# Product of probabilities and V over 64 rows at once, with V's second arrangement laid out by DMA

## The chip, the cores and the metric

One Trainium2 (trn2) chip, one of its cores. The metric is device time in microseconds (us) from the start to the end of one execution of the whole kernel.

## What is computed

The program is a chain of layers over `x` of 16 sequences x 256 tokens x 128 channels: an opening stage (a scan with an orthogonal product), a transformer of six layers, a multi-query attention, a state-space stage and a mixture of experts. Only the transformer is touched. The part of it around the change, cut to what matters:

```python
WINDOW, HEADS, DIM_HEAD, DEPTH = 32, 16, 64, 6
def local_attention(q, k, v):          # b, h, n, d ; n = 256 tokens
    bq, bk, bv = (t.reshape(b, h, n // 32, 32, d) for t in (q, k, v))
    look = lambda t: concat([block before (zeros ahead of the first), the block itself], axis=3)
    sim = einsum('bhwie,bhwje->bhwij', bq, look(bk)) * 8.0
    sim = where(it < jb or it > jb + 32 or no such block, -big, sim)
    return einsum('bhwij,bhwje->bhwie', softmax(sim), look(bv))
def attn_layer(x):                     # q, k: l2norm, rotary; v plain
    return local_attention(q, k, v) @ Wo
# each layer: x + attn_layer(shift_tokens(x)), then x + a gated feed-forward of 341 hidden columns
```

So each block of 32 queries looks at 64 keys: its own block of 32 and the one before it.

## The kernel before, in words

The transformer stage (`transformer_stage`, lines 780 to 1485) works on tiles of 128 tokens: 6 layers x 16 sequences x 2 tiles = 192 tiles. Sequence number and layer make a unit `U` (96 of them), `t` is the tile of a unit (0 is the even tile, 1 the odd one). The work is a software pipeline of steps, written out by hand in one `body` for each engine, in the same order of steps on all (`all_steps`, line 770). In step k tile k is projected to q and k, tile k-1 is turned, tile k-2 has its scores and V, tile k-3 its product with V, tile k-4 its output projection. Every fourth step ends a pair of units, and the feed-forward of an earlier pair is spread over the four steps (`ff`, 0 to 3). Everything is f32; a matmul in f32 is two instructions in the trace, each with a weight load of its own.

TensorE's order in a step (line 1207): `project(step, 0)` (L1071), with ff = 1 `turn_xn`, `scores` (L1102, L1112), with ff = 3 `widen(step, 2)`, `turn_probs` (L1053), `output` (L1167), `project(step, 1)`, `turn_part(step, 0)` (L1053, eight transposes of q), `attend(step, 0)`, `turn_part(step, 1)` (eight transposes of k), `attend(step, 1)`, `project_v` (L1087), in odd steps `turn_input`, and last `widen(step, 0)` with ff = 1, `widen(step, 1)` with ff = 2 (both L1189) or `narrow` with ff = 3 (L1203).

`attend` (line 1123) is what the change is about. V of a tile lies with its blocks of 32 keys in four places: block 2m + parity of the odd or even heads in partitions 64 odd + 32 parity, slot m. `V` has four such slots of tiles in a ring (`v_slot`, line 700), filled by ScalarE from PSUM (`keep_v`, L1275). The matmuls take 32 rows (the keys of one block), 64 weight columns (V's channels of one head) and 64 or 32 moving columns (the queries that look at this block), and add in the two PSUM banks `mixed`, which two bf16 matmuls with zero weights (L1131) clear first. `attend(step, 0)` does the blocks of parity 0, `attend(step, 1)`, after a wait for the first to be done, those of parity 1 and, in odd tiles, the last block of the tile before:

```python
windows = [(0, 0), (2, 0)]                                    # parity 0: 64 columns each
windows = [(1, 0), (3, 0)] + ([(3, 1)] if t else [])          # parity 1: 64, 32 (and 32) columns
r = slice(64 * odd + 32 * parity, 64 * odd + 32 * parity + 32)
```

ScalarE's order in a step (line 1319) ends with: `copy_part(step, 0)` (L1283), `square(step, 1)` (L1264), `copy_part(step, 1)` (L1283), `keep_out` (L1298: the result of `attend`, after both parities), `inverse_norm` (L1269, L1271), `keep_v` (L1275), in odd steps `copy_input` (L1259), then a gelu. `widen` with j < 2 and `narrow` write to the same banks `mixed` and so wait for `keep_out` (lines 1184 and 1195); the next step's `scores` wait for `keep_v`.

SyncE issues all DMAs of the stage from one queue in program order (lines 859 to 988): for each unit `residual(U)` (a wait for tile 2U-3's sum, then three shifting copies in SBUF, L897 to L899, and a load, L891) and `unit(U)` (weights at layer ends, `load_input` L886 to L888, every second unit `save_pair` L904).

Of the kernel before, what the change touches and what calls it, by code (L numbers as in the profile page):

```python
# [11 lines left out]
ACT = mybir.ActivationFunctionType  # L12
AX = mybir.AxisListType
F32 = mybir.dt.float32
BF16 = mybir.dt.bfloat16

P = 128
B = 16
T = 256
TT = T // P  # L20
# [641 lines left out]
PAIRS = HEADS // 2  # L662
# [24 lines left out]
class Step:  # L687
# [11 lines left out]

    def v_slot(self, lag):  # L700

        return (self.k - lag) % 4

# [76 lines left out]
def transformer_stage(k, z):  # L780

    nc, d = k.nc, k.dram
    with ExitStack() as ctx:
# [13 lines left out]
        identb = sb("identb", [P, P], BF16)  # L797
        zerob = sb("zerob", [P, P], BF16)

# [10 lines left out]
        kT = sb("kT", [P, PAIRS, WIN + T])  # L810
        V = sb("V", [P, 4, WPT // 2, PAIRS, HD])
        prob = sb("prob", [P, TT, PAIRS, 2, HD])
# [36 lines left out]
        clamped, logged, rn_ready = (ev(n) for n in "clamped logged rn_ready".split())  # L849
        v_done, v_kept, pv_done = ev("v_done"), ev("v_kept"), ev("pv_done", 2)  # L850
        scored, maxed, centred, exped, den_sum, den_inv, prob_ready, o_copied, out_done, z_added = (
# [7 lines left out]
        def _(sp):  # L859
            for e in (zu_ready, zr_ready[0], zr_ready[1], zsh_ready, z_saved, q_ok, k_ok, v_ok, out_ok, ff_ok):  # L860
                e.start(sp)
# [28 lines left out]
            def load_residual(u, p):  # L890
                sp.dma_start(zr[:, p, :, :], z[:, bass.ds(u * TT, TT), :]).then_inc(zr_ready[p].sem, 16)  # L891

            def shift_output(U, unit):
# [36 lines left out]
            def unit(U):  # L930


                nonlocal loads
                l, i, J = U // B, U % B, U // 2 - 2
                if i == B - 1 and l + 1 < DEPTH:
                    sp.wait_ge(roped.sem, roped.at(U * 2 + 1, 1))
                    load_columns(l + 1, 0)
                    load_table(l + 1, 0)
                    loads += 2
                    sp.wait_ge(weights, 16 * loads)  # L940
                sp.sem_inc(q_ok.sem, 1)
                if i == B - 1 and l + 1 < DEPTH:
                    sp.wait_ge(roped.sem, roped.at(U * 2 + 1, 2))
                    load_columns(l + 1, 1)
                    load_table(l + 1, 1)
                    loads += 2
                    sp.wait_ge(weights, 16 * loads)
                sp.sem_inc(k_ok.sem, 1)
                if i == 0 and l:
                    sp.wait_ge(v_done.sem, v_done.at(U * 2 - 1, 1))  # L950
                    load_columns(l, 2)
                    loads += 1
                    sp.wait_ge(weights, 16 * loads)
                if U:
                    sp.sem_inc(v_ok.sem, 1)
                if U + 2 <= UNITS:
                    sp.wait_ge(filled, place(Step(U * 2 // LOOP, U * 2 % LOOP + 1), "input") + 1)
                    load_input((i + 2) % B)
                if i % 2 and J >= 0:
                    save_pair(J % (B // 2), J)  # L960
                    if i == 3 and l:
                        load_ff_weights(l)
                        loads += 4
                        sp.wait_ge(weights, 16 * loads)
                    sp.sem_inc(ff_ok.sem, 1)
# [11 lines left out]

            for U in range(UNITS):
                if U >= 2:
                    residual(U)  # L980
                unit(U)
            for i in range(2):
                shift_output(UNITS + i - 2, i + 2)
                sp.sem_inc(out_ok.sem, 1)
# [62 lines left out]
        def _(pe):  # L1047
# [74 lines left out]

            def attend(step, parity):

                tau, t = step.tile(3), step.t(3)
                if parity == 0:
                    pe.wait_ge(copied, place(step, "p") + 2)
                    pe.wait_ge(v_kept.sem, v_kept.at(tau, 1))
                    pe.wait_ge(z_added.sem, z_added.at(tau - 1, 1))
                    for odd in range(2):  # L1130
                        nc.tensor.matmul(mixed[:, odd, 0:1], zerob[:, :], identb[:, 0:1],  # L1131
                                         start=True, stop=False, skip_group_check=True)
                    windows = [(0, 0), (2, 0)]
                else:
                    pe.wait_ge(pv_done.sem, pv_done.at(tau, 1))
                    windows = [(1, 0), (3, 0)] + ([(3, 1)] if t else [])
                for j in range(PAIRS // 2):
                    for v, back in windows:
                        lo, hi = (0, WIN) if back else (v * WIN, min(v + 2, WPT) * WIN)
                        for half in range(2):  # L1140
                            for odd in range(2):
                                r = slice(64 * odd + 32 * parity, 64 * odd + 32 * parity + 32)
                                pair = j + 4 * half
                                last = nc.tensor.matmul(mixed[64 * half:64 * half + 64, odd, j * P + lo:j * P + hi],  # L1144
                                                        V[r, step.v_slot(3 + back), v // 2, pair, :],
                                                        probT[r, t, pair, lo:hi],
                                                        start=False, stop=True, skip_group_check=True)
                last.then_inc(pv_done.sem, 1)
# [58 lines left out]
            def body(step):  # L1207
# [19 lines left out]
                if step.has(3):  # L1227
                    attend(step, 0)
                if step.has(1):
                    turn_part(step, 1)  # L1230
                if step.has(3):
                    attend(step, 1)
                if step.has(2):
# [10 lines left out]
            pe.wait_ge(zeroed, 5)  # L1244
            pe.wait_ge(masks_ready, 5)
            turn_input(0, 0)
# [4 lines left out]
        def _(act):  # L1251
# [20 lines left out]

            def keep_v(step):
                act.wait_ge(v_done.sem, v_done.at(step.tile(2), 1))
                nc.scalar.activation(V[:, step.v_slot(2), :, :, :].rearrange("p m a e -> p (m a e)"), flat2(score), ACT.Copy)\  # L1275
                    .then_inc(v_kept.sem, 1)
# [19 lines left out]
            def keep_out(step):  # L1296
                act.wait_ge(pv_done.sem, pv_done.at(step.tile(3), 2))
                nc.scalar.activation(oT[:, step.t(3), :, :], flat2(mixed).rearrange("p (a c) -> p a c", a=PAIRS),  # L1298
                                     ACT.Copy).then_inc(o_copied.sem, 1)
# [60 lines left out]
        def _(dve):  # L1360
# [6 lines left out]
            nc.vector.memset(eps[:, :], LN_EPS).then_inc(masks_ready, 1)  # L1367
            nc.vector.memset(zerob[:, :], 0.0).then_inc(masks_ready, 1)
            nc.vector.memset(ss[:, :, :, 1:2], 1e-24).then_inc(masks_ready, 1)
# [1456 lines left out]
```

## Time and profile before

| | us |
|---|---|
| median of 3 runs (lowest, highest) | 4871.99 (4866.45, 4878.07) |
| the profiled execution, its own time | 4863.11 |
| its span, first to last instruction | 4861.4 |
| TensorE (PE) busy | 4421.3 (91%) |
| VectorE (DVE) busy | 3153.7 (65%) |
| ScalarE (ACT) busy | 2729.3 (56%) |
| GpSimd (POOL) busy | 2625.0 (54%) |

The profile is of one execution. "Busy" is the union of an engine's instructions; PE is its matmuls, PEld its weight loads, which overlap them. Ends of matmuls are modelled, so a distance between two bursts is read from start to start. The transformer takes about the stretch from 200 to 3600 us of the span.

### The profile page before, as it was taken

The page shows a single profiled execution, that of the slowest core. Times are in us where ns is not written, and L with a number is a line of the kernel's source. Part 1 is how long each engine was busy: PE and PEld are TensorE (multiplying, and loading weights), DVE is VectorE, ACT ScalarE, POOL GpSimd, SP SyncE. Part 2 cuts the span into 40 slices and gives each one's busy share as a digit, 9 for nine tenths or more (in the row PEclk, how much of TensorE's full clock was granted, in tenths as well). Part 3 has the DMA queues.
Part 4 walks back from the last instruction along what each step waited for, and adds up shares of the span by engine and source line. Part 5 has one row for each costly group of instructions (what it writes and reads, how often), then busy time and mean ns, then how long its engine had stood idle before and what let it go on. Part 6 is the DMA issues. An engine that isn't in the chain of part 4 may idle for free. (4 is left out here: it accounts for less than half of the span.)

```text
span 4861.4 us, 165534 instructions
## 1 busy us (share of the span) xinstructions
PE 4421.3 (91%) x72708; PEld 2877.1 (59%) x72708; DVE 3153.7 (65%) x4106; ACT 2729.3 (56%) x3932; POOL 2625.0 (54%) x1465
## 2 busy tenths in 40 slices
PE   7489999999999999999999999999957999788868
PEld 5256666666666666666666666666634554344435
DVE  3477776767667676677666666667633333699964
ACT  4256665666566666656656665656632343577733
POOL 0266666666566665666656665666622111577742
PEclk8699999999999999999999999999987898899989
DMA  2100001000100001100010001100010000211100
GB/s 54 51 11 18 17 20 37 25 15 20 28 26 22 20 17 32 27 20 18 22 33 23 19 17 33 28 18 16 19 38 12 5 4 1 93 79 77 70 16 16
DMA packets 186590, 136.07 MB, mean 28 GB/s; under 512 B 122410, under 2 KB 172595, under 8 KB 183795
## 3 DMA queue, kind: packets, MB, share of 16 engines
q1 hardware_dynamic: 185843, 125.10, 8.6%
q8 instruction: 592, 9.70, 0.8%
q14 instruction: 155, 1.27, 0.1%
HBM read 68.51 MB, written 4.03 MB: 15 GB/s over the span
## 5 line engine op out<-in xcount | busy, mean ns | idle before, releaser
L1005 POOL TENSOR_TENSOR tf_qk<-tf_qk,tf_rot 128x1024 f32<-128x1024 f32 x384 | 908.7, 2366 | 1214.4 <-DVE tf_rot L1388 1214.4
L1071 PE MATMUL tf_psum<-tf_Wqkv,tf_xsT 128*128 128x512 f32 x1536 | 747.7, 610 | 66.2 <-issue 44.6
L1012 POOL TENSOR_TENSOR tf_qk<-tf_qk,tf_rn 128x1024 f32<-128x1024 f32 x384 | 724.2, 1912 | 55.3 <-ACT tf_rn L1271 55.3
L1264 ACT ACTIVATE tf_sq<-tf_psum 128x1024 f32<-128x1024 f32 x384 | 393.4, 1024 | 530.7 <-DVE tf_rot L1388 530.7
L1384 DVE TENSOR_TENSOR tf_qk<-tf_psum,tf_table 128x1024 f32<-128x1024 f32 x384 | 467.4, 1217 | 263.2 <-PE tf_psum L1071 262.6
L1144 PE MATMUL tf_psum<-tf_probT,tf_V 32*64 32x64 f32 (+1 forms) x27648 | 493.5, 219 | 7.2 <-issue 6.6
L1071 PEld LDWEIGHTS tf_psum<-tf_Wqkv,tf_xsT 128*128 128x128 f32 x1536 | 274.0, 194 | 349.0 <-issue 338.6
L1394 DVE TENSOR_REDUCE tf_ss<-tf_sq 128x16 f32<-128x1024 f32 x384 | 457.5, 1191 | 21.8 <-ACT tf_sq L1264 21.8
L1144 PEld LDWEIGHTS tf_psum<-tf_probT,tf_V 32*64 32x64 f32 x27648 | 442.8, 133 | 45.8 <-issue 41.0
L1388 DVE TENSOR_TENSOR tf_rot<-tf_psum,tf_table 128x1024 f32<-128x1024 f32 x384 | 465.8, 1213 | 0.0
L1053 PE MATMUL tf_psum<-ident,tf_qk 128*128 128x128 f32 x3072 | 409.5, 276 | 3.4 <-ACT tf_qT L1283 2.4
L1053 PEld LDWEIGHTS tf_psum<-ident,tf_qk 128*128 128x128 f32 x3072 | 344.0, 142 | 102.9 <-issue 82.2
L1447 DVE SCALAR_TENSOR_TENSOR tf_hT<-tf_psum,tf_b,tf_gel 128x512 f32<-128x512 f32 x144 | 107.4, 746 | 436.5 <-ACT tf_gel L1316 436.5
L1167 PE MATMUL tf_psum<-tf_Wo,tf_oT 128*128 128x128 f32 x3072 | 376.4, 275 | 8.2 <-issue 5.2
L1167 PEld LDWEIGHTS tf_psum<-tf_Wo,tf_oT 128*128 128x128 f32 x3072 | 362.3, 192 | 33.4 <-issue 22.9
L1020 POOL TENSOR_TENSOR tf_prob<-tf_prob,tf_rden 128x1024 f32<-128x1024 f32 x192 | 367.0, 1911 | 13.0 <-DVE tf_rden L1418 13.0
L1087 PE MATMUL tf_psum<-tf_Wqkv,tf_xsT 128*32 128x512 f32 x3072 | 369.6, 598 | 0.0
L1283 ACT ACTIVATE tf_qT<-tf_psum 128x1024 f32<-128x1024 f32 x192 | 196.4, 1023 | 282.0 <-PE tf_psum L1053 282.0
L2024 POOL TENSOR_TENSOR mb_read<-mb_state,mb_Csb 128x1024 f32<-128x1024 f32 x128 | 300.2, 2356 | 76.5 <-DVE mb_state L2267 57.0
L1112 PEld LDWEIGHTS tf_psum<-tf_kT,tf_qT 64*32 64x32 f32 x24576 | 261.0, 105 | 108.3 <-issue 108.0
L1112 PE MATMUL tf_psum<-tf_kT,tf_qT 64*32 64x64 f32 x24576 | 296.8, 226 | 20.6 <-issue 20.4
L2107 PE MATMUL mb_psum<-mb_read,ident 128*128 128x512 f32 x512 | 251.8, 615 | 59.3 <-POOL mb_read L2024 48.4
(313 smaller groups left out, 7542.0 us busy)
## 6 DMA issues: line engine op xcount, KB each, us to landing
mb_Csb<-mb_kept SPq DMA_DIRECT2D x16, 2048.0 KB, 7.1
tf_zr<-z SPq DMA_DIRECT2D x96, 128.0 KB, 2.7
z<-tf_z SPq DMA_DIRECT2D x48, 256.0 KB, 2.5
tf_Wqkv<-in_Wqkv_split SPq DMA_DIRECT2D x18, 512.0 KB, 3.7
tf_zu<-z SPq DMA_DIRECT2D x97, 64.0 KB
tf_zu<-z SPq DMA_DIRECT2D x97, 63.5 KB
tf_zsh<-tf_z SPq DMA_DIRECT2D x96, 64.0 KB
tf_zsh<-tf_z SPq DMA_DIRECT2D x96, 63.5 KB
```

The source lines that it names most:

```text
L1005: nc.gpsimd.tensor_tensor(v, v, rot[:, kind, :], ALU.add).then_inc(added.sem, 1)
L1012: nc.gpsimd.tensor_tensor(v, v, rn[:, t, HEADS * kind:HEADS * (kind + 1)].unsqueeze(2) .to_broadcast([P, HEADS, HD]), ALU.mult).then_inc(n ...
L1053: last = nc.tensor.transpose(flat2(trans)[:, j * P:(j + 1) * P], source(j), k.ident[:, :])
L1071: last = nc.tensor.matmul(proj[:, half, :], xsT[:, step.unit(0), WIN + t * P:WIN + (t + 1) * P], Wqkv[:, c:c + 512], start=True, stop=True)
L1087: last = nc.tensor.matmul(score[r:r + 32, m, :], xsT[:, step.unit(2), x:x + WIN], Wqkv[:, c:c + 512], start=True, stop=True)
L1112: last = nc.tensor.matmul(score[w * WIN:(w + 1) * WIN, odd, pair * HD:(pair + 1) * HD], qT[r, t, pair, w * WIN:(w + 1) * WIN], keys, start ...
L1144: last = nc.tensor.matmul(mixed[64 * half:64 * half + 64, odd, j * P + lo:j * P + hi], V[r, step.v_slot(3 + back), v // 2, pair, :], probT ...
L1167: last = nc.tensor.matmul(mixed[:, 0, 0:P], oT[:, t, pair, :], Wo[:, pair, :], start=(pair == 0), stop=(pair == PAIRS - 1))
L1264: nc.scalar.activation(sq[:, kind, :], flat2(proj), ACT.Square).then_inc(squared.sem, 1)
L1384: nc.vector.tensor_tensor(qk[:, t, kind, :].rearrange("p (h e) -> p h e", e=HD), v, cos, ALU.mult)
L1388: nc.vector.tensor_tensor(rot[:, kind, :].rearrange("p (h a e) -> p h a e", a=2, e=HD // 2), swapped, sin, ALU.mult).then_inc(roped.sem, 1)
L1394: nc.vector.tensor_reduce(ss[:, t, HEADS * kind:HEADS * (kind + 1), 0], sq[:, kind, :].rearrange("p (h e) -> p h e", e=HD), AX.X, ALU.add)\
```

## The change

Each block of queries now gets one matmul over both of its blocks of keys, 64 rows with 32 moving columns, written to PSUM at once instead of added there. For odd blocks of queries the two blocks of keys already lie side by side in `V`. For even ones a second arrangement, `Vback`, is filled by DMA from `V`: SyncE copies the rows of the block itself and, shifted by one slot, those of the block before (four DMAs for an even tile, six for an odd one: two of 128 KB, two or four of 64 KB). The first block of a sequence (w = 0, t = 0) has no block before it and keeps a matmul of 32 rows. The order of the probabilities' halves is as it was (the mask rolls them for even blocks). `V` has two slots in place of four, `Vback` two. The two halves of `attend` become one, between the two `turn_part`s. One bf16 matmul with the identity as weights stands ahead of it in place of two with zeros.

```diff
-        V = sb("V", [P, 4, WPT // 2, PAIRS, HD])
+        V, Vback = (sb(n, [P, TT, WPT // 2, PAIRS, HD]) for n in ("V", "Vback"))
...
+            def lay_back(tau):
+                t = tau % 2
+                sp.wait_ge(v_kept.sem, v_kept.at(tau, 1))
+                sp.wait_ge(pv_done.sem, pv_done.at(tau - 2, 1))
+                for odd in range(2):
+                    even_rows, odd_rows = (slice(64 * odd + i, 64 * odd + i + WIN) for i in (0, WIN))
+                    sp.dma_start(Vback[even_rows, t, :, :, :], V[even_rows, t, :, :, :]).then_inc(laid[t].sem, 16)
+                    sp.dma_start(Vback[odd_rows, t, 1, :, :], V[odd_rows, t, 0, :, :]).then_inc(laid[t].sem, 16)
+                    if t:
+                        sp.dma_start(Vback[odd_rows, 1, 0, :, :], V[odd_rows, 0, 1, :, :]).then_inc(laid[1].sem, 16)
...
                 if U:
                     sp.sem_inc(v_ok.sem, 1)
+                if U:
+                    lay_back(U * 2 - 1)
                 if U + 2 <= UNITS:
...
             for U in range(UNITS):
+                if U:
+                    lay_back(U * 2 - 2)
                 if U >= 2:
                     residual(U)
                 unit(U)
+            lay_back(TILES - 2)
+            lay_back(TILES - 1)
...
-            def attend(step, parity):
+            def attend(step):
...
+                pe.wait_ge(copied, place(step, "p") + 2)
+                pe.wait_ge(laid[t].sem, laid[t].at(step.unit_of(3), 96 if t else 64))
+                pe.wait_ge(z_added.sem, z_added.at(tau - 1, 1))
+                nc.tensor.matmul(mixed[:, 0, 0:1], identb[:, :], identb[:, 0:1], start=True, stop=True)
                 for j in range(PAIRS // 2):
-                    for v, back in windows:
-                        lo, hi = (0, WIN) if back else (v * WIN, min(v + 2, WPT) * WIN)
+                    for w in range(WPT):
+                        alone = w == 0 and t == 0
+                        source = Vback if w % 2 == 0 and not alone else V
                         for half in range(2):
                             for odd in range(2):
-                                r = slice(64 * odd + 32 * parity, 64 * odd + 32 * parity + 32)
-                                pair = j + 4 * half
-                                last = nc.tensor.matmul(mixed[64 * half:64 * half + 64, odd, j * P + lo:j * P + hi],
-                                                        V[r, step.v_slot(3 + back), v // 2, pair, :],
-                                                        probT[r, t, pair, lo:hi],
-                                                        start=False, stop=True, skip_group_check=True)
+                                r = slice(64 * odd, 64 * odd + (WIN if alone else 2 * WIN))
+                                pair, at = j + 4 * half, w * WIN
+                                last = nc.tensor.matmul(mixed[64 * half:64 * half + 64, odd, j * P + at:j * P + at + WIN],
+                                                        source[r, t, w // 2, pair, :], probT[r, t, pair, at:at + WIN],
+                                                        start=True, stop=True)
                 last.then_inc(pv_done.sem, 1)
...
                 if step.has(3):
-                    attend(step, 0)
+                    attend(step)
                 if step.has(1):
                     turn_part(step, 1)
-                if step.has(3):
-                    attend(step, 1)
...
             def keep_v(step):
+                t = step.t(2)
                 act.wait_ge(v_done.sem, v_done.at(step.tile(2), 1))
+                act.wait_ge(laid[1 - t].sem, laid[1 - t].at(step.unit_of(3), 64 if t else 96))
+                act.wait_ge(pv_done.sem, pv_done.at(step.tile(4), 1))
```

## Rows read from the trace of the kernel before

**Rows 1.** The page: the span, then busy time of each engine.
```profile
span 4861.4 us, 165534 instructions
...
PE 4421.3 (91%) x72708; PEld 2877.1 (59%) x72708; DVE 3153.7 (65%) x4106; ACT 2729.3 (56%) x3932; POOL 2625.0 (54%) x1465
```

**Rows 2.** Busy time by stretch, four of 700 us from 600 to 3400: their sum.
```profile
sum 2800.00, PE 2720.90 PEld 1872.19 DVE 1944.13 ACT 1703.77 POOL 1738.87; mean PE 680.23 PEld 468.05 DVE 486.03 ACT 425.94 POOL 434.72
```

**Rows 3.** Waits, PE alone, 600 to 3400: who, for whom, us in total, times, longest.
```profile
PE tf_psum L1071 <- issue: 25.1, 10, 3.5
...
PE tf_psum L1131 <- DVE tf_z L1429: 15.2, 41, 0.4
```

**Rows 4.** Groups by form, whole span: rows*columns of weights, moving operand, count | busy, mean ns.
```profile
L1144 PE MATMUL tf_psum<-tf_probT,tf_V 32*64 32x64 f32 x18432 | 451.0, 224 | 3.5 <-issue 3.3
...
L1144 PE MATMUL tf_psum<-tf_probT,tf_V 32*64 32x32 f32 x9216 | 238.1, 209 | 3.7 <-issue 3.2
...
L1131 PE MATMUL tf_psum<-tf_identb,tf_zerob 128*128 128x1 bf16 x384 | 36.6, 165 | 18.0 <-DVE tf_z L1429 18.0
```

**Rows 5.** Timeline of PE, parts of three steps: start us, length us, what, count.
```profile
2026.08 1.09 PE L1053 MATMUL tf_psum<-ident,tf_qk 128*128 128x128 f32 x8
2027.10 1.60 PE L1144 MATMUL tf_psum<-tf_probT,tf_V 32*64 32x64 f32 x96
2028.63 1.92 PE L1087 MATMUL tf_psum<-tf_Wqkv,tf_xsT 128*32 128x512 f32 x16
...
2036.93 1.95 PE L1167 MATMUL tf_psum<-tf_Wo,tf_oT 128*128 128x128 f32 x16
2038.72 1.88 PE L1071 MATMUL tf_psum<-tf_Wqkv,tf_xsT 128*128 128x512 f32 x4
...
2041.43 1.16 PE L1144 MATMUL tf_psum<-tf_probT,tf_V 32*64 32x64 f32 x64
2042.59 1.09 PE L1053 MATMUL tf_psum<-ident,tf_qk 128*128 128x128 f32 x8
2043.61 1.13 PE L1144 MATMUL tf_psum<-tf_probT,tf_V 32*64 32x64 f32 x64
2044.67 1.92 PE L1087 MATMUL tf_psum<-tf_Wqkv,tf_xsT 128*32 128x512 f32 x16
2046.53 0.44 PE L1053 MATMUL tf_psum<-ident,tf_zu 128*128 128x128 f32 x2
...
2048.52 1.88 PE L1071 MATMUL tf_psum<-tf_Wqkv,tf_xsT 128*128 128x512 f32 x4
2050.24 0.59 PE L1102 MATMUL tf_psum<-tf_mask,tf_identb 128*128 128x512 bf16 x2
```

**Rows 6.** Timeline of PE in the later stage of multi-query attention.
```profile
4000.06 0.40 PE L1653 MATMUL mq_psum<-mq_bv,mq_ones 1*128 1x32 f32 x2
4000.40 0.41 PE L1652 MATMUL mq_psum<-mq_Wv,mq_hT 128*128 128x32 f32 x2
4000.74 0.40 PE L1653 MATMUL mq_psum<-mq_bv,mq_ones 1*128 1x32 f32 x2
```

**Rows 7.** Timeline of ACT in the step of rows 5, and PE's next product.
```profile
2044.03 1.02 ACT L1283 ACTIVATE tf_kT<-tf_psum 128x1024 f32<-128x1024 f32 x1
2044.94 1.03 ACT L1298 ACTIVATE tf_oT<-tf_psum 128x1024 f32<-128x1024 f32 x1
...
2046.66 1.02 ACT L1275 ACTIVATE tf_V<-tf_psum 128x1024 f32<-128x1024 f32 x1 [0.31 <-PE tf_psum L1087]
...
2057.71 1.16 PE L1144 MATMUL tf_psum<-tf_probT,tf_V 32*64 32x64 f32 x64
```

**Rows 8.** DMA: two issues on SyncE's queue, and the page's line on `zr` (KB, landing).
```profile
2007.61 0.65 SPq L897 DMA_DIRECT2D tf_zsh<-tf_z  x1
...
2009.05 2.92 SPq L899 DMA_DIRECT2D tf_zsh<-tf_z  x1
...
tf_zr<-z SPq DMA_DIRECT2D x96, 128.0 KB, 2.7
```

More of the change, by code:

```diff
@@ L698, in t, with unit_of @@
         return (self.k - lag) % TT
-    def v_slot(self, lag):
-        return (self.k - lag) % 4
+    def unit_of(self, lag):
+        return self.I * (LOOP // 2) + (self.k - lag) // 2
     def unit(self, lag):
@@ L797, in transformer_stage @@
         identb = sb("identb", [P, P], BF16)
-        zerob = sb("zerob", [P, P], BF16)
         zu = sb("zu", [P, TT, P])
@@ L849, in transformer_stage @@
         clamped, logged, rn_ready = (ev(n) for n in "clamped logged rn_ready".split())
-        v_done, v_kept, pv_done = ev("v_done"), ev("v_kept"), ev("pv_done", 2)
+        v_done, v_kept, pv_done, laid = ev("v_done"), ev("v_kept"), ev("pv_done"), [ev("laid0", 64), ev("laid1", 96)]
         scored, maxed, centred, exped, den_sum, den_inv, prob_ready, o_copied, out_done, z_added = (
@@ L859, in _ @@
         def _(sp):
-            for e in (zu_ready, zr_ready[0], zr_ready[1], zsh_ready, z_saved, q_ok, k_ok, v_ok, out_ok, ff_ok):
+            for e in (zu_ready, zr_ready[0], zr_ready[1], laid[0], laid[1], zsh_ready, z_saved, q_ok, k_ok, v_ok, out_ok, ff_ok):
                 e.start(sp)
@@ L1121, in turn_probs @@
                 turn(PAIRS, lambda j: prob[:, t, j, :, :].rearrange("p b e -> p (b e)")).then_inc(filled, 1)
-            def attend(step, parity):
+            def attend(step):
                 tau, t = step.tile(3), step.t(3)
[L1126 to L1136, printed above, removed]
+                pe.wait_ge(copied, place(step, "p") + 2)
+                pe.wait_ge(laid[t].sem, laid[t].at(step.unit_of(3), 96 if t else 64))
+                pe.wait_ge(z_added.sem, z_added.at(tau - 1, 1))
+                nc.tensor.matmul(mixed[:, 0, 0:1], identb[:, :], identb[:, 0:1], start=True, stop=True)
@@ L1244, in _ @@
             pe.wait_ge(zeroed, 5)
-            pe.wait_ge(masks_ready, 5)
+            pe.wait_ge(masks_ready, 4)
             turn_input(0, 0)
@@ L1273, in keep_v @@
             def keep_v(step):
+                t = step.t(2)
                 act.wait_ge(v_done.sem, v_done.at(step.tile(2), 1))
-                nc.scalar.activation(V[:, step.v_slot(2), :, :, :].rearrange("p m a e -> p (m a e)"), flat2(score), ACT.Copy)\
+                act.wait_ge(laid[1 - t].sem, laid[1 - t].at(step.unit_of(3), 64 if t else 96))
+                act.wait_ge(pv_done.sem, pv_done.at(step.tile(4), 1))
+                nc.scalar.activation(V[:, t, :, :, :].rearrange("p m a e -> p (m a e)"), flat2(score), ACT.Copy)\
                     .then_inc(v_kept.sem, 1)
@@ L1296, in keep_out @@
             def keep_out(step):
-                act.wait_ge(pv_done.sem, pv_done.at(step.tile(3), 2))
+                act.wait_ge(pv_done.sem, pv_done.at(step.tile(3), 1))
                 nc.scalar.activation(oT[:, step.t(3), :, :], flat2(mixed).rearrange("p (a c) -> p a c", a=PAIRS),
@@ L1367, in _ @@
             nc.vector.memset(eps[:, :], LN_EPS).then_inc(masks_ready, 1)
-            nc.vector.memset(zerob[:, :], 0.0).then_inc(masks_ready, 1)
             nc.vector.memset(ss[:, :, :, 1:2], 1e-24).then_inc(masks_ready, 1)
```

## Prediction

> **What bounds the kernel now.** I read the page first: TensorE is busy 91% of the span, the next engine, VectorE, 65% [rows 1]. An average over stages can mislead, so the busy times by stretch come next: in the middle of the transformer PE is busy 2720.9 of 2800 us, the others at most 1944.1 [rows 2]. The waits say what the missing 79 us are: the longest is 25.1 us before a projection with no releaser, the second that matters here 15.2 us before L1131, for the sum of the tile before [rows 3]; neither is touched. So nearly every us taken from PE's own sequence in this stage leaves the total, and every us added to it arrives there. The other engines count only where PE would have to wait for them.
>
> **What the product with V costs today.** L1144 has 27,648 instructions in two forms, 18,432 with 64 moving columns and 9,216 with 32 [rows 4]; over 192 tiles that is 128 in an even tile (64 + 64) and 160 in an odd one (64 + 96). The timeline gives the time from start to start: first burst 2041.43 to 2042.59 = 1.16 us for 64, second burst of an even tile 2043.61 to 2044.67 = 1.06 us for 64, of an odd tile 2027.10 to 2028.63 = 1.53 us for 96 [rows 5]. The last two differ by 32 instructions and 0.47 us: 14.7 ns for one. What is left is a fixed part for each burst, 1.06 - 64 x 0.0147 = 0.12 us; for the first burst, all of 64 columns and followed by transposes, it is 1.16 - 0.94 = 0.22 us. The 32 instructions by which the odd burst is longer have 32 moving columns, and the second burst of an even tile is half made of these, yet none is cheaper: the count of instructions matters, not their columns.
>
> **What the change removes.** All tiles get 4 x 4 x 4 = 64 matmuls, 128 instructions, and one burst in place of two. As one unbroken burst that is 128 x 0.0147 + 0.22 = 2.10 us, with the larger fixed part because transposes follow it too. Before it was 1.16 + 1.06 = 2.22 us (even) and 1.16 + 1.53 = 2.69 us (odd). Gain 0.12 + 0.59 = 0.71 us for each of 96 units, 68 us; with the smaller fixed part 0.20 us more, 87 us. One bf16 matmul less (L1131, two per tile before [rows 4]) is worth about 1 us in all, since two of them follow each other without a gap that the rows could show. That weights now fill 64 rows instead of 32 I cost at nothing: scores run with 64 rows, and L1167 with 128 rows and 128 columns takes 1.79 us for 16 instructions, 112 ns for one [rows 5], the rate of loading 128 columns one after the other; four tiles of 64 columns at 4 x 14.7 = 59 ns fit half of that. Writing with start=True instead of adding: nothing; both are one write of the same columns.
>
> **What it adds on PE.** The first block of a sequence keeps 32 rows. In an even tile the loop over j goes 8 instructions of 32 rows, 24 of 64 rows, four times over: eight short bursts in place of one, that is seven more changes of how the array is divided. Does such a change cost the fixed part of a burst? No row shows 32*64 beside 64*64. But wherever rows or columns of the tile change, the trace pays. The bias product alternates 128*128 and 1*128, and one pair starts every 0.34 us [rows 6]; a pair of L1167 needs 2 x 0.112 = 0.22 us, so a change costs 0.12 us. V's projection (four at once, 128*32) runs 1.86 us to the next start where four rounds of a 512-column product are 4 x 0.43 = 1.72 us by L1071 (1.72 us for four): 0.14 us [rows 5]. The bursts of L1144 give 0.12 and 0.22. I take 0.13, the middle of the three small ones, since no change inside the loop has the 64-column stream or the transposes of the 0.22. Cost 7 x 0.13 = 0.91 us, x 96 = **87 us**; bounds 0 (no drain) and 7 x 0.22 x 96 = 148 us.
>
> The Trainium skill, "TensorEngine Tiling (Array Packing)", section Key Properties, says that changing the tiling mode, and not just the tile, drains TensorE, and its list of configurations has 32x64 and 64x64 as separate ones. By that rule the change costs what the other kinds of change do; without it the sum would be the 87 us smaller. No row here shows this pair.
>
> **What it adds around PE.** ScalarE: `keep_out` (L1298) could start as the second parity ended, at about the end of the copy of k (2044.03 and 2044.94, [rows 7]). Now the transposes of k come after the whole product and V's projection right behind them. Counted from the first transpose of k: the transposes last 1.09 us [rows 5], the copy starts at an estimated 1.13, `keep_out` 0.91 later (the distance in rows 7), ends 1.02 later at 3.06, and is seen by PE at about 3.12. PE is through V's projection at 1.02 + 1.86 = 2.88 [rows 5]. With ff = 2 `widen` then waits 0.24 us, 48 times: **12 us**. With ff = 1 and 3 the turning of the input (about 0.3 us) covers it; without that cover they would cost the like, 36 us in all. Below nothing isn't possible. `keep_v` moves some 0.7 us later, behind `keep_out` and L1269 and L1271; the next scores wait for it, covered by a projection of 1.7 us.
>
> SyncE's queue: ten DMAs more per unit, 960 in all, and 86 MB. The last product of an odd tile may start only when six have landed. `keep_v` ended at 2047.68 and the next product started at 2057.71 [rows 7]: 10.0 us, 9.3 after the shift. An issue takes 0.65 us [rows 8], landing of 128 KB 2.7 us: 6 x 0.65 + 2.7 = 6.6 us. Cost nothing, 2.7 us to spare (3.9 for an even tile with four). Behind them in the queue stands `load_input`, up to 4 us later, which has a whole step before anyone wants it; `save_pair` likewise; `residual` comes mid-step, long after. ScalarE's new waits in `keep_v` are for what PE's product has already waited for. The price of a copy from SBUF to 32 rows of SBUF isn't in the trace: bounds 0.65 us each in the queue, and 2.92 us as L899 behind a copy of 127 rows [rows 8].
>
> The Trainium skill, "SBUF — State Buffer", section on the DMA port swizzle, states that 32 partitions reach 8 of 16 ports and measured 189 GB/s. By it the 512 KB of an odd tile are an estimated 2.8 us, less than their issues; that would leave the sum as it is.
>
> **Sum.** -68 - 1 + 87 + 12 = +30 us on the profiled execution's 4863.1, so 4893. The median of the runs shown lies 8.9 us above that execution; on it the forecast is **4902 us**, 0.6% slower. Ends: -87 + 7 x 0.12 x 96 (81) + 0 = -6, and -68 + 148 + 36 = +116, both together unlikely; its own range 4880 to 4970. A difference of 0.2%, 10 us, is about what a measurement of this kernel tells from none.
>
> **Rivals.** (1) *Mixed rows don't drain.* 32 and 64 rows with the same 64 columns may count as one division, since the four tiles begin at the same rows and columns. For it: every change seen also switched the columns, or to or from the whole array. Against: that of the bias product [rows 6] keeps 128 columns and costs 0.12. Then -69 + 12 = -57: 4815 us, faster. It decides between 32*64 and 64*64 alone; break-even is 57 / (7 x 96) = 0.085 us a change. Chance 0.17. (2) *The layout comes late.* If each copy blocks the queue like L899, six take 17.5 + 2.7 = 20 us, 11 too late in every odd tile and 6 in every even one: over 1000 us. It begins when six take more than 9.3 us, 1.1 us each; at 1.3 us it is +1.2 us per unit, 5000 us or more. Against: L899's row follows a copy that no engine shares evenly. 0.06. (3) *64 rows load or run slower*, say by 10%: 0.2 us more per tile, 38 us, 4940. 0.04. (4) That the change doesn't do what it says (few matmuls less): the counts follow from the loops, 27,648 to 24,576; nothing speaks for it.
>
> **How the numbers follow.** The likeliest case, bursts that drain, has 0.73: inside it the result is more than 10 us slower in 0.61, within 10 us in 0.11, faster in 0.01. Rival 1 adds 0.16 faster and 0.01 same, rivals 2 and 3 add 0.10 slower. Faster 0.17, same 0.12, slower 0.71. The likeliest case less its tails and rival 3 hold under 8 in 10, so the range takes in rival 1: 4808 to 4965.
>
> **What would show it.** L1144's line in the new profile should have two forms, 32*64 with 3072 instructions (4 x 4 x 2 x 96) and 64*64 with 21,504. On PE's timeline an even tile's product should show as groups of 8 and 24, 0.25 and 0.48 us apart, some 2.9 us from first matmul to first transpose; an odd one as one burst of 2.1. PE should wait for ACT's L1298 before L1189, about 12 us. No wait for the DMA of `Vback`. I am wrong if even tiles too take 2.1 us (rival 1), if PE waits for a DMA before L1131 (rival 2), or if an odd tile's burst is well over 2.1 (rival 3).

## The result, and the profile after

The kernel with the change took 4919.08 us, the median of 4 runs (4913.82 to 4926.24), beside 4872.96 us (4 runs) for the one before: a ratio of 1.0096, 95% interval 1.0078 to 1.0115. That is 46 us or 1.0% slower; 4902 was forecast, with a range of 4808 to 4965. The direction and the range held. Below, the sum behind them turns out to hold three wrong terms.

The page of the kernel after, its span and busy times, and two of its DMA queues (packets, MB, share of 16 engines):

```profile
span 4915.2 us, 160659 instructions
...
PE 4464.3 (91%) x69444; PEld 2883.6 (59%) x69444; DVE 3153.8 (64%) x4105; ACT 2712.6 (55%) x3932; POOL 2625.0 (53%) x1465
...
q1 hardware_dynamic: 231923, 213.24, 16.5%
q8 instruction: 557, 9.13, 0.8%
```

Beside [rows 1], PE has 3264 matmul instructions fewer and is busy 43 us longer; ScalarE has 17 us less to do, the other engines are where they were. The page before has 125.10 MB on q1, so the ten copies per unit add 88 MB (86 had been forecast). Busy time of the stretches of [rows 2], their granted clock in the column behind POOL, for the kernel after:

```profile
600.00:1300.00 700.00, 679.76 (x13341) 463.12 (x13340) 479.56 (x607) 418.08 (x518) 430.85 (x219) 0.99 0.20 48
...
2000.00:2700.00 700.00, 682.06 (x13200) 464.20 (x13199) 478.34 (x605) 415.29 (x513) 427.94 (x218) 0.98 0.20 49
...
sum 2800.00, PE 2722.97 PEld 1854.15 DVE 1918.51 ACT 1668.77 POOL 1720.70; mean PE 680.74 PEld 463.54 DVE 479.63 ACT 417.19 POOL 430.18
```

PE is as full as before (2720.9) while DVE, whose work per step is the same, has 1.3% less to do in these 2800 us: fewer steps fit in. Little of the loss is waiting; PE's own sequence became longer. PE's waits in the same stretch, where [rows 3] stood:

```profile
PE tf_psum L1088 <- issue: 21.8, 10, 2.7
PE tf_psum L1146 <- DVE tf_z L1439: 17.0, 40, 0.8
PE tf_psum L1129 <- issue: 14.8, 11, 1.8
PE tf_psum L1199 <- ACT tf_oT L1309: 10.7, 40, 0.3
```

The fourth row is new, and is the wait for `keep_out` that was forecast. It was forecast at 12 us; over the whole span it is 13.5. None for a DMA of `Vback` is there. The forms of the product, where [rows 4] stood:

```profile
L1155 PE MATMUL tf_psum<-tf_probT,tf_V 64*64 64x32 f32 x12288 | 404.0, 222 | 4.2 <-issue 3.8
...
L1155 PE MATMUL tf_psum<-tf_probT,tf_Vback 64*64 64x32 f32 x9216 | 305.4, 220 | 0.2 <-issue 0.2
L1155 PE MATMUL tf_psum<-tf_probT,tf_V 32*64 32x32 f32 x3072 | 122.0, 228 | 1.3 <-issue 1.3
```

3072 of one and 21,504 of the other: the change does what it says. PE's timeline, an odd tile and then an even one (a row that names `V` may hold instructions of both forms, where they follow each other):

```profile
2009.64 0.32 PE L1155 MATMUL tf_psum<-tf_probT,tf_Vback 64*64 64x32 f32 x8
...
2011.64 1.09 PE L1070 MATMUL tf_psum<-ident,tf_qk 128*128 128x128 f32 x8
2012.66 1.92 PE L1104 MATMUL tf_psum<-tf_Wqkv,tf_xsT 128*32 128x512 f32 x16
2014.85 1.95 PE L1199 MATMUL tf_psum<-tf_xnT,tf_W 128*128 128x512 f32 x4 [0.27 <-ACT tf_oT L1309]
...
2028.00 0.56 PE L1155 MATMUL tf_psum<-tf_probT,tf_V 32*64 32x32 f32 x16
2028.39 0.30 PE L1155 MATMUL tf_psum<-tf_probT,tf_Vback 64*64 64x32 f32 x8
2028.50 0.79 PE L1155 MATMUL tf_psum<-tf_probT,tf_V 64*64 64x32 f32 x24
2029.12 0.30 PE L1155 MATMUL tf_psum<-tf_probT,tf_Vback 64*64 64x32 f32 x8
...
2029.96 0.92 PE L1155 MATMUL tf_psum<-tf_probT,tf_V 64*64 64x32 f32 x24
...
2031.23 1.97 PE L1070 MATMUL tf_psum<-ident,tf_qk 128*128 128x128 f32 x8
2033.13 2.26 PE L1104 MATMUL tf_psum<-tf_Wqkv,tf_xsT 128*32 128x512 f32 x16
```

The odd burst lasts 2009.64 to 2011.64 = 2.00 us, where 2.10 was forecast. In the even tile a round of 32 instructions repeats every 0.73 us (2028.39 to 2029.12), not the 0.47 of 32 in one run. The end of this tile shows something unforeseen: the transposes that take 1.02 us at 2011.64 take 1.90 at 2031.23. The granted clock says why, in a window before and one around it:

```profile
2028.00:2030.00 2.00, 2.00 (x93) 1.79 (x94) 1.64 (x3) 1.47 (x2) 2.00 (x2) 1.00 0.14 33
2030.00:2034.00 4.00, 4.00 (x68) 2.92 (x64) 0.94 (x2) 0.76 (x1) 1.87 (x2) 0.57 0.19 52
```

1.00 is the level of 2.4 GHz; 0.57 over 4 us is about 3.4 us at 1.2 GHz. I count such falls between 600 and 3400 us in the records of the granted clock: 7 of them, 27 us, before; 18, 61 us, after.

Where I speak below of **the product's time**, it is from the first matmul with V of each burst to the start of what PE does next, summed over all bursts of the span; **the scores' time** is the same for the bursts of `scores`. Before: 485.7 and 306.0 us. After: 486.1 and 312.0. So the merged bursts and the mixed rows cancelled to 0.4 us, and the 46 us are elsewhere. The same count for PE's other bursts says where, for the two profiled executions: the transposes of q and k went from 393.3 to 411.5, V's projection from 356.4 to 381.7 (the wait for `keep_out` and the low clock), the output projection from 352.2 to 357.8, the scores up by 6, the turning of the input from 47.7 to 53.7, `narrow`, the last part of the feed-forward, down by 7.

### The profile page after: what moved, and what is told of

It reads as the page before. It is cut to its first block and busy times, and to the rows that moved or that the text cites. A ratio compares the mean times of both kernels' runs of the same rounds, so it can differ in the third digit from the quotient of the medians.

```text
span 4915.2 us, 160659 instructions
## 1 busy us (share of the span) xinstructions
PE 4464.3 (91%) x69444; PEld 2883.6 (59%) x69444; DVE 3153.8 (64%) x4105; ACT 2712.6 (55%) x3932; POOL 2625.0 (53%) x1465
## 5 line engine op out<-in xcount | busy, mean ns | idle before, releaser
L1155 PE MATMUL tf_psum<-tf_probT,tf_V 64*64 64x32 f32 (+1 forms) x15360 | 478.8, 224 | 5.5 <-issue 5.1
L1155 PEld LDWEIGHTS tf_psum<-tf_probT,tf_V 64*64 64x64 f32 (+1 forms) x15360 | 409.9, 134 | 39.3 <-issue 5.1
L1070 PE MATMUL tf_psum<-ident,tf_qk 128*128 128x128 f32 x3072 | 422.4, 282 | 5.0 <-issue 2.6
L1104 PE MATMUL tf_psum<-tf_Wqkv,tf_xsT 128*32 128x512 f32 x3072 | 379.5, 613 | 0.0
L1294 ACT ACTIVATE tf_kT<-tf_psum 128x1024 f32<-128x1024 f32 x192 | 196.5, 1024 | 249.5 <-PE tf_psum L1070 249.5
```

What stands on the lines that cost most here:

```text
L1070: last = nc.tensor.transpose(flat2(trans)[:, j * P:(j + 1) * P], source(j), k.ident[:, :])
L1294: nc.scalar.activation(dst, src, ACT.Copy).then_inc(copied, 1)
```

## The experiments

Ratios are against the kernel before on the same chip, with their 95% intervals. Diffs are against the kernel after unless said otherwise.

**Mixed rows grouped.** In an even tile the order of the blocks becomes all 32-row ones first: one change between forms instead of seven.

```
+blocks = [(j, w) for w in range(WPT) for j in range(PAIRS // 2)] if t == 0 else \
+    [(j, w) for j in range(PAIRS // 2) for w in range(WPT)]
-for j in range(PAIRS // 2):
-    for w in range(WPT):
+for j, w in blocks:
```

> The changed kernel with the blocks of even tiles in another order: first the four groups of 32 rows, then all of 64 rows, so one change of the array's division inside the product in place of seven. Theory (each change costs 0.131 us, 0.915 us per even tile): even product 2.914 - 6 x 0.131 = 2.13 us, 75 us less in 96 tiles, so 4919 - 75 = 4844 us or somewhat under. Rival (the broken product also makes the granted clock fall, 18 short falls in 600 to 3400 against 7 before): the falls go back to about 7 and the gain is 90 to 100 us, 4820 to 4830. Rival (the loss lies in the DMAs or in ScalarE's later copies): under 20 us gained, 4900 or more.

Measured: 4840.34 us, 0.9933 (0.9914 to 0.9952), which is faster than the kernel before. Its timeline has an even tile's product as:

```profile
2019.56 1.26 PE L1156 MATMUL tf_psum<-tf_probT,tf_V 32*64 32x32 f32 x64
2020.64 0.65 PE L1156 MATMUL tf_psum<-tf_probT,tf_Vback 64*64 64x32 f32 x32
2021.11 0.65 PE L1156 MATMUL tf_psum<-tf_probT,tf_V 64*64 64x32 f32 x32
```

The median even product is 2.129 us, against 2.914 in the kernel after and 1.999 for the odd one. One change costs 2.129 - 1.999 = 0.130 us, seven cost 2.914 - 1.999 = 0.915, 0.131 each. The price is for the change, not for the 32-row instructions.

**First block with zeros.** The block without a forerunner takes 64 rows too, the upper 32 of which are zeros in `Vback`, set once.

```
-alone = w == 0 and t == 0
+alone = False
...
+nc.vector.memset(Vback[WIN:2 * WIN, 0, 0, :, :], 0.0).then_inc(masks_ready, 1)
+nc.vector.memset(Vback[3 * WIN:4 * WIN, 0, 0, :, :], 0.0).then_inc(masks_ready, 1)
```

> The changed kernel without any block of 32 rows: the first block of a sequence takes 64 rows too, the missing 32 being zeros set once, and its probabilities for them are zero. Theory (0.131 us per change, 7 changes): both tiles' products take 2.00 us, 88 us less, 4919 - 88 = 4831 us, 0.99 of the kernel before or a little less. Rival (clock falls tied to the broken product): 4805 to 4815. Rival (DMAs or ScalarE): 4900 or more.

Measured: 4838.66 us, 0.9917 (0.9889 to 0.9945). Both products have a median of 1.999 us and their time falls from 486.1 to 402.0: the seven changes had cost 84 us of PE's time, and the run is 80 us shorter. With 64 rows an instruction still starts every 14.6 ns (127 in 1.849 us), so Rival 3 is out too.

**32 rows in odd tiles too** (the half of the previous block is left out there): the changes of form twice as often.

```
-alone = w == 0 and t == 0
+alone = w == 0
```

> The changed kernel with the suspected cost doubled: w = 0 takes 32 rows in odd tiles as well, so that their product too is broken in eight (the part of the block before is left out there). Theory (0.131 us per change): the odd product goes from 2.00 to 2.91 us, 88 us more, 4919 + 88 = 5007 us. If the clock falls follow the broken products, their number doubles from 18 and 20 us more are lost, 5027. Rival (32 rows cost by themselves and not by the change): the added time is the same in each group of 8, but a single group of 32-row blocks as in the grouped order would then also stay at 2.91.

Measured: 4983.52 us, 1.0221 (1.0185 to 1.0256). The product's time rose by 82 us to 568.5, as the theory has it, both medians at 2.914; the total rose by only 64, where 88 were expected (the two intervals leave 20 us either way, and the traced execution, 5003 us, is the longest of the four). The scores' time gave 16 back (312.0 to 296.0), most of it in their waits:

```profile
PE tf_psum L1129 <- issue: 2.2, 2, 1.3
```

where the kernel after has 14.8. "issue" is a wait that nothing in the profile releases. When the product is slow, the burst of `scores` that follows later runs without such stalls. This was a first sign, not yet more, that PE's dense bursts are also limited by something other than PE.

**`keep_out` first.** ScalarE empties the product's bank before it copies the turned k.

```
-if step.has(1):
-    copy_part(step, 1)
 if step.has(3):
     keep_out(step)
+if step.has(1):
+    copy_part(step, 1)
```

> The changed kernel with ScalarE copying the product out before it copies the turned k, instead of after. Theory (TensorE waits for this copy, 0.34 us before the feed-forward's second part in 47 steps and 0.06 us in 93 more): the waits for L1309 vanish and 20 to 23 us are gained, 4897 us. Rival (the copy of k comes late instead, for the turning of the input or the next scores): the same wait moves to another line, no gain, 4919.

Measured: 4892.55 us, 1.0037 (1.0021 to 1.0054), 27 us less than the kernel after. No row for L1309 is left among PE's waits, and V's projection to `widen` takes 1.854 us again instead of 2.190. ScalarE in the kernel after and then in this one, from the copy of k on:

```profile
2012.77 1.02 ACT L1294 ACTIVATE tf_kT<-tf_psum 128x1024 f32<-128x1024 f32 x1 [0.40 <-PE tf_psum L1070]
2013.69 1.02 ACT L1309 ACTIVATE tf_oT<-tf_psum 128x1024 f32<-128x1024 f32 x1
```

```profile
2020.86 1.03 ACT L1309 ACTIVATE tf_oT<-tf_psum 128x1024 f32<-128x1024 f32 x1 [1.69 <-PE tf_psum L1155]
2021.85 1.02 ACT L1294 ACTIVATE tf_kT<-tf_psum 128x1024 f32<-128x1024 f32 x1
```

With the old order `keep_out` ends at 2014.71, 3.07 us after PE began the transposes of k at 2011.64 (3.06 was forecast), and PE goes on at 2014.85, where V's projection was through at 2014.51 (2012.66 + 1.85). The steps into `widen` lose 47 x 0.336 = 16 us, and the 93 steps where a turning of the input lies between lose 0.062 each, 6 us: 22 in all. The measured 27 agrees within the intervals, which leave some 12 us either way.

**Both mends together**, the zeros and `keep_out` first.

> The two repairs together: no block of 32 rows (zeros in the missing rows) and ScalarE copying the product out before the turned k. Theory (the two costs are separate and add): 0.9917 less the 0.5% of the second repair, 0.986 to 0.987 of the kernel before, some 4812 us; the waits for the copy of the product vanish. Rival (once the broken product is gone the wait hides under something else): no better than 0.9917, 4839.

Measured: 4802.35 us, 0.9846 (0.9830 to 0.9861): 1.5% under the kernel before, and no version that computes the reference is faster by more than the intervals. On 4873 that is 4798; with the zeros alone it was 4833, so the order of ScalarE is worth 35 us here, with an interval of about 15 either way. PE's timeline shows 22 between these two versions as well: V's projection 373.9 to 358.1 us, the turning of the input 54.1 to 47.7.

**The second arrangement left out.** As the one above, without `lay_back` and its waits; the product reads `V` in place of `Vback`, so that even blocks multiply the wrong block of keys and the result is not the reference's.

```
-                    lay_back(U * 2 - 1)
...
-                    lay_back(U * 2 - 2)
...
-                        source = Vback if w % 2 == 0 and not alone else V
+                        source = V
```

> The same kernel with both repairs, without the second arrangement: no DMA of it, no wait for it, and the product takes V for even blocks too (whose rows are then the wrong block of keys). Theory (the 86 MB of copies disturb TensorE, whose scores took a median of 1.50 us instead of 1.42 with them): the scores go back to 1.42 us, 16 us less than the kernel with both repairs. Rival (the copies cost nothing, the scores are longer because the instructions before them are others): scores stay at 1.50 and the time is the same within 5 us.

Measured: 4760.09 us, 0.9761 (0.9741 to 0.9782). The same matmuls and no wait for a copy in either, and still 42 us less. The scores' time is 291.0 us here and 319.3 with the copies; the product's is the same (402.8 and 402.0). Waits before the scores between 600 and 3400, without the copies and then with them:

```profile
PE tf_psum L1123 <- issue: 8.7, 11, 1.2
```

```profile
PE tf_psum L1129 <- issue: 17.8, 24, 1.6
```

One of the latter on the timeline, with the copies; the 98 and the 30 are one burst of 128, and nothing stands between the two but the gap:

```profile
2001.55 1.19 PE L1129 MATMUL tf_psum<-tf_kT,tf_qT 64*32 64x64 f32 x98
2004.06 0.45 PE L1129 MATMUL tf_psum<-tf_kT,tf_qT 64*32 64x64 f32 x30 [1.32 <-issue]
```

Most of the cost is less visible: the median burst of scores takes 1.53 us with the copies and 1.42 without. Its 81st instruction starts 0.795 us into the burst in both, the last at 1.381 and 1.269. With the copies PE slows down late in a burst, when it has run through many short instructions in a row. The scores are 28 of the 44 us between the two profiled executions. Another 6.7 are a wait of another kind, which the kernel after has too:

```profile
PE tf_psum L1177 <- SPq L1001: 6.7, 1, 6.7
```

It comes once, at the end of the stage: the signal for the last output projections stands in SyncE's queue behind `lay_back(TILES - 1)`. Every version with the copies has this wait, at 5.4 to 10.2 us, and neither the kernel before nor the one without the layout has it. Some 7 more are two waits of 3.5 and 3.8 us for new weights, which this execution has and the kernel after has not; the traces with merged and with doubled copies have such waits too, the others none.

**Every copy issued twice**, the second time into a tile that nobody reads.

```
+sp.dma_start(spare[even_rows, t, :, :, :], V[even_rows, t, :, :, :]).then_inc(laid[t].sem, 16)
+sp.dma_start(spare[odd_rows, t, 1, :, :], V[odd_rows, t, 0, :, :]).then_inc(laid[t].sem, 16)
...
```

> The kernel with both repairs with each copy of the second arrangement issued once more, to a spare tile, so twice the DMAs and bytes. Theory (copies disturb TensorE): 16 us more again, and twelve issues at 0.65 us plus landing are 10.5 us against 9 of cover in odd tiles, up to 1.5 us of waiting in each of 96 units, so 16 to 160 us more. Rival (copies cost nothing as long as they are in time): only the waiting, if twelve take more than 9 us, else no change.

Measured: 4926.69 us, 1.0106 (1.0083 to 1.0129), 124 us over the version with the copies once. Here the layout does come late:

```profile
PE tf_psum L1150 <- DMA tf_spare<-tf_V: 52.3, 39, 3.0
```

That is 52 of these 2800 us and 56.5, 42 times, over the whole span; the scores' time rises once more, by 8, the product's by 12, and the granted clock is at half for 89 us between 600 and 3400, where the version with the copies once has 34. With twice the work on the queue it is late for 39 of about 160 products, by up to 3.0 us. Rival 2 was real, only its point lies beyond the ten copies.

**The kernel before, with the ten copies added** into a spare tile. ScalarE's `keep_v` waits for them as in the kernel after, PE doesn't (a diff against the kernel before; `s` is the tile's slot of the four).

```
+sp.dma_start(spare[even_rows, t, :, :, :], V[even_rows, s, :, :, :]).then_inc(laid[t].sem, 16)
...
```

> The kernel before the change, product and all as it was, with the change's ten copies per unit added on SyncE's queue at the same places, into a tile that nobody reads. Theory (the copies by themselves slow TensorE's instructions by about 42 us, as much as leaving them out gave back): 4879 + 42 = 4921 us, ratio 1.007 to 1.010, scores from 1.42 to about 1.50 us. Rival (they cost only beside the unbroken product, which draws instructions for longer): no more than 10 us.

Measured: 4922.76 us, 1.0092 (1.0077 to 1.0107), 0.0092 x 4873 = 45 us for copies whose data nobody reads, with the old product. The scores' time is 329.9 (306.0 before), the product's 494.4 (485.7), and the wait of 6.7 us at the end of the stage is there. Its waits between 600 and 3400, where the kernel before has 17.9 and 5.3:

```profile
PE tf_psum L1134 <- issue: 28.0, 26, 1.8
...
PE tf_psum L1166 <- issue: 9.8, 19, 1.2
```

**Half the bytes**, in as many copies: only pairs 0 to 3 of each; for pairs 4 to 7 the product with `Vback` is left at zero. **Eight copies instead of ten**, the same bytes: the two shifted copies of an odd tile as one.

```
+half = slice(0, PAIRS // 2)
...
-sp.dma_start(Vback[even_rows, t, :, :, :], V[even_rows, t, :, :, :]).then_inc(laid[t].sem, 16)
+sp.dma_start(Vback[even_rows, t, :, half, :], V[even_rows, t, :, half, :]).then_inc(laid[t].sem, 16)
...
```

```
+flat = lambda x: x.rearrange("p t m a e -> p (t m) (a e)")
...
-sp.dma_start(Vback[odd_rows, t, 1, :, :], V[odd_rows, t, 0, :, :]).then_inc(laid[t].sem, 16)
-if t:
-    sp.dma_start(Vback[odd_rows, 1, 0, :, :], V[odd_rows, 0, 1, :, :]).then_inc(laid[1].sem, 16)
+to, of = (slice(2, 4), slice(1, 3)) if t else (slice(1, 2), slice(0, 1))
+sp.dma_start(flat(Vback[odd_rows, :, :, :, :])[:, to, :], flat(V[odd_rows, :, :, :, :])[:, of, :]).then_inc(laid[t].sem, 16)
```

> The kernel with both repairs (zero rows, the product copied out first) with copies of half the columns: the same ten DMAs per unit, half the bytes, 43 MB (for half the heads the even blocks then multiply zeros). Theory (bytes on the DMA engines are what disturbs TensorE): half of the 42 us come back, 4781 us. Rival (it is the number of DMAs or of packets on SyncE's queue): nothing comes back, 4802.

> The kernel with both repairs, the two shifted copies of an odd tile issued as one of 128 KB: eight DMAs per unit in place of ten, the same bytes, the same result. Theory (bytes): the same time within 5 us, 4802. Rival (number of DMAs): a fifth of 42 us comes back, 4794.

Measured: 4787.61 us, 0.9826 (0.9812 to 0.9839), and 4801.64 us, 0.9837 (0.9819 to 0.9854), where the version with ten whole copies has 0.9846. Half the bytes give back about 10 us of the 42 (0.0020 of the ratio), but the intervals leave anything from 0 to 20; half of 42 would be 21. Fewer issues give 4 us, with 11 either way, so the 8 us of a fifth are not excluded. Most likely the bytes alone do not carry the whole cost; whether it goes by bytes, by issues or by something else, these two runs don't decide.

**The product in two halves** around the transposes of k, as the kernel before had it, with the zeros and ScalarE's old order.

```
 if step.has(3):
-    attend(step)
+    attend(step, 0)
 if step.has(1):
     turn_part(step, 1)
+if step.has(3):
+    attend(step, 1)
```

> The kernel with zeros in the missing rows, ScalarE in its old order, and the product cut in two halves of 64 instructions around the turning of k, as the product was placed before. Theory (a burst costs 0.13 us beside its instructions): 192 x 0.13 = 25 us more than unbroken, and no wait for the copy of the product, so 25 us above the kernel with both repairs, 4837. Rival (what was gained came from the placing of the turning and not from the count of instructions and bursts): no better than before, 4870.

Measured: 4820.39 us, 0.9883 (0.9863 to 0.9903), 18 us over the best version. There is no wait for L1309. The product's time is 31 us more (433.2), 0.16 us for each of 192 extra bursts, and the scores' 12 less. The halves are alike, 64 instructions with 32 columns each, but the first takes a median of 1.18 us to the transposes of k and the second 1.07 us to V's projection. Keeping the burst whole and mending ScalarE's order is better than cutting it.

## Why the forecast was right, and what in it was wrong

The versions make a chain in which each link undoes one part of the change. Ratios times 4873 us:

| from | to | what differs | us | forecast |
|---|---|---|---|---|
| before, 4873 | no second layout, 4757 | one burst, fewer matmuls, no changes of form | -116 | -69 |
| 4757 | both mends, 4798 | the copies | +41 | 0 |
| 4798 | zeros alone, 4833 | ScalarE's order | +35 | +12 |
| 4833 | after, 4920 | seven changes between forms | +87 | +87 |

The sum is +47, the +46 observed; that the links close is no check, since each starts where the last one ends, and each is uncertain by 10 to 16 us. The forecast's was +30. That it came so close is in part luck: a gain was taken 47 us too small and two costs 64 us.

- **Bound by PE:** right. 84 us of PE's time taken away by the zeros shortened the run by 80.
- **Mixed rows cost:** right, and the price to the digit: 0.13 taken, 0.131 measured. It was chosen from changes of other kinds [rows 5, 6]; the grouped version shows it for this kind by itself. Rival 1 is out. That the link is 87 us as well is partly chance: the medians of the two versions differ by 80, the product's time by 84, and in the traces the transposes of q and k (398.3 to 411.5) and V's projection (373.9 to 381.7) grow by 21 more, while the scores and `narrow` shrink by 18. The Trainium skill, "TensorEngine Tiling (Array Packing)", section Key Properties, has the rule that changing the mode drains TensorE; the price of 0.131 us a change agrees with it, also where only the rows change from 32 to 64.
- **The gain of one burst:** mis-sized. The step "2.10 us, with the larger fixed part because transposes follow it too" failed: the burst takes 2.00, 128 x 0.0147 + 0.12. The 0.22 read off the first burst was not all fixed part: it held a wait too short for the profile's list of waits. In the kernel before, 144 of the 190 first bursts are followed by the transposes of k 0.05 to 0.15 us after ScalarE has ended its copy of q, for which PE's code waits there; in the other 46 the copy had ended earlier, and the transposes start 0.15 us after the last product instruction, as they do behind the unbroken burst. In the step of [rows 5] the copy ends at 2042.53, and the transposes start at 2042.59:

```profile
2041.51 1.02 ACT L1283 ACTIVATE tf_qT<-tf_psum 128x1024 f32<-128x1024 f32 x1 [1.76 <-PE tf_psum L1053]
```

  The product in two halves, with 32 columns everywhere, has the same split, 144 and 46, so the columns are not the reason either. The unbroken burst outlasts the copy and hides it. That makes the product -83 us (485.7 to 402.8), near the 87 given as the other end. A further 15 us came from the scores (306.0 to 291.0), which the sum had no term for, and 5 from the clearing matmuls (23.2 to 18.4), forecast at 1. The rest of the 116 is not assigned: the two profiled executions are only 97 us apart.
- **ScalarE's order:** right in mechanism and place, mis-sized. Forecast: a wait of 0.24 us, 48 times, and the turning of the input covers it in the other steps. Measured: 0.34 us 47 times, and the cover fell short by 0.06 us in 93 steps. 22 us can be seen on PE's timeline both times, 27 and 35 us by undoing it; the intervals cover the difference.
- **The copies:** the term that failed. "Cost nothing" was argued from when they land, and for the product that was right: PE waits for none of them in the kernel after, and the layout is late in earnest only when doubled. But being in time is not being free. They cost 41 us without the old product and 45 with it. Most of that is slower bursts on PE and short stalls in them, 28 and 33 us in the scores and the product. 6.7 us are a wait for SyncE's queue at the end of the stage, where what stands behind the copies is wanted at once; the forecast had looked at the queue in the middle of the stage only. No bound for either stood in it: both of its bounds, 0.65 and 2.92 us a copy, were of the issue, which takes a median of 0.59 us.
- **The granted clock:** not foreseen. 11 more falls and 34 us more at half speed are about 17 us of lost work. They fit the mixed rows: 6 falls when grouped, 7 with zeros, 27 in the version with broken products in every tile; and 11 of the 18 in the kernel after begin in a burst of the product, where none of the 7 before do, nor any when grouped or with zeros. But versions without any mixed rows have 7 to 14 falls, 5 of the 14 in the product, and the one with doubled copies, where PE waits, has 19, 12 of them there. So the mixed rows are not the only thing that brings them. The table's last link contains whatever they cost; their cause stays open.

**What stays open about the copies.** The late slowing within a burst and the stalls look like the supply of instructions running short: PE has 69,444 matmul instructions and as many weight loads, and the page counts a queue of kind "instruction", q8, on the same 16 DMA engines as the copies. The stalls do go with that queue. Between 600 and 3400 us the kernel before has 37 stalls without a releaser before or in a burst of scores or product, and all 37 end 2.0 to 3.4 us after a packet of q8 has begun; at the 91st instruction of the 214 such bursts without a stall, that is so for 50. The same holds for all 15 in the version without the copies, all 30 with both mends, and all 45 in the kernel before with the copies added. So the copies doubled the stalls in one pair and raised them from 37 to 45 in the other; the kernel after, with its slow product, has 15. The packets of q8 took 1144 ns on average without the copies and 1171 with both mends, 1081 before and 1157 with the copies added, a small step for such an effect. For the late slowing of bursts without a stall there is no such tie: in the kernel before, 58% of the 43 slow ones (last instruction later than 1.33 us) and 56% of the 95 others have a packet within some 3 us. A coincidence in time is not yet a cause; no run changed the supply alone.

## What to carry to other kernels

A transfer inside SBUF that nobody waits for is not free beside an engine that runs thousands of short instructions: price it by adding it, unused, to the kernel before. Order matmuls so that tiles of one shape stand together, or pad the odd one with zeros; each change of shape here costs as much as nine matmul instructions. When two bursts become one, look at who empties their bank and in which order, since what was hidden behind the second burst no longer is. And before a remainder is called the fixed part of a burst, look at what another engine ended just then: it may be a wait too short to be listed.

## What the runs showed that I had not expected

- Ten copies per unit, 88 MB in the run, cost 41 to 45 us although PE hardly ever waits for one. Of 128 instructions in a burst of scores, the first 80 keep their pace (0.795 us in both), the last starts 0.11 us later. Every stall in these bursts ends 2.0 to 3.4 us after a packet of the instruction queue has begun.
- A wait of PE for SyncE's queue of 6.7 us appeared at the end of the stage, where the last signal stands behind the last copies.
- The larger fixed part of the old product's first burst held a wait of 0.06 to 0.15 us for ScalarE's copy of q, hidden again by the unbroken burst.
- A change between 32-row and 64-row tiles with the same 64 columns costs 0.130 us once and 0.131 us each when there are seven.
- PE's granted clock falls to half for about 3.4 us at a time in a stage where it is busy 97% of the time, 6 to 27 times in 2800 us. In the kernel after no wait of PE in this stretch is longer than 2.7 us; why the count differs between versions isn't shown.
